# Quantised attention on one core: a projection's shift behind the exponentials on ACT, its clipping behind the rounding of the probabilities on DVE

## The reference, cut to what matters

```python
def _fq(x, delta, zp, n_bits):
    xi = _round_ste(x / delta) + zp
    xq = jnp.clip(xi, 0.0, 2.0 ** n_bits - 1.0)
    return (xq - zp) * delta
q = (x @ wq)...; k = (ctx @ wk)...; v = (ctx @ wv)...
sim = einsum(_fq(q, dq, 128.0, 8), _fq(k, dk, 128.0, 8)) * SCALE
attn = softmax(sim)
out = einsum(_fq(attn, dw, 0.0, 8), _fq(v, dv, 128.0, 8)) @ wo + bo
```

## Time and profile before

| | |
|---|---|
| time, median of 3 runs | 3130.22 us (3127.51 to 3131.3) |
| the profiled execution's own time | 3129.03 us |
| its span | 3127.2 us |
| PE busy | 2829.2 us, 90% |
| DVE busy | 1832.3 us, 59% |
| ACT busy | 1449.7 us, 46% |
| POOL busy | 706.1 us, 23% |
| L674 maximum | x256, mean 1219 ns |
| L688 scaling | x1024, mean 347 ns |
| L696 rounding | x256, mean 691 ns |
| L585 exponentials | x1024, mean 563 ns |
| L555 shift | x192, mean 778 ns |

### The profile page before, as it was taken

The page is one execution under the profiler, slowest core; times in us unless marked ns, Lnnn a source line. Parts: engine busy times, 40 slices in busy tenths (PEclk is TensorE's granted clock), DMA queues, the critical chain, the costliest instruction groups (busy, mean ns, idle before and its releaser), DMA issues. The chain is left out here.

```text
span 3127.2 us, 54588 instructions
## 1 busy us (share of the span) xinstructions
PE 2829.2 (90%) x18304; PEld 2274.0 (73%) x18304; DVE 1832.3 (59%) x4469; ACT 1449.7 (46%) x3747; POOL 706.1 (23%) x1147
## 2 busy tenths in 40 slices
PE   3689989989998886499999997999999999999997
PEld 2555666666565663289999997888888888888886
DVE  4599999999999997543333334334443344434332
ACT  3466677777667775321111112444444444444442
POOL 0122222222222222133333332111112111111110
PEclk8799999999999998699999998999999999999997
DMA  5133333333333333230000003000000000000000
GB/s 149 39 73 77 77 77 83 80 78 77 77 77 84 77 78 68 71 112 27 35 32 27 27 32 116 35 27 34 27 27 34 27 27 27 27 27 27 34 14 14
DMA packets 328217, 168.59 MB, mean 54 GB/s; under 512 B 276960, under 2 KB 293344, under 8 KB 328160
## 3 DMA queue, kind: packets, MB, share of 16 engines
q1 hardware_dynamic: 328160, 167.87, 21.1%
HBM read 75.54 MB, written 25.17 MB: 32 GB/s over the span
## 5 line engine op out<-in xcount | busy, mean ns | idle before, releaser
L585 ACT ACTIVATE e<-S,bias,qk_scale 128x256 f32<-128x256 f32 x1024 | 563.5, 563 | 106.9 <-DVE pq L696 100.2
L674 DVE TENSOR_REDUCE negmax<-S 128x4 f32<-128x1024 f32 x256 | 311.9, 1219 | 64.2 <-PE S L494 63.9
L688 DVE TENSOR_SCALAR e<-e,rsum 128x256 f32<-128x256 f32 x1024 | 291.0, 347 | 2.9
L555 ACT ACTIVATE shifted<-PJ,round_col,inv 128x512 f32<-128x512 f32 x192 | 149.2, 778 | 230.9 <-PE PJ L162 230.8
L153 PE MATMUL PJ<-w_a_wo,oT 128*128 128x512 f32 x512 | 243.7, 621 | 2.6 <-ACT oT L594 1.8
L1560 POOL TENSOR_TENSOR mid_partsB<-mid_actB,mid_partsB 128x256 fp32r<-128x256 f32 x128 | 101.4, 792 | 637.7 <-DVE mid_partsB L1465 637.7
L162 PE MATMUL PJ<-hT,w_a_wq 128*128 128x256 f32 x1536 | 202.7, 289 | 23.4 <-DVE w_a_wq L415 19.8
L162 PEld LDWEIGHTS PJ<-hT,w_a_wq 128*128 128x128 f32 x1536 | 190.5, 194 | 36.2 <-issue 36.2
L585 ACT ACTIVATION_READ_ACCUMULATOR e<-S,bias,qk_scale 128x1 f32 x1024 | 207.5, 203 | 0.0
L162 PE MATMUL AG0A<-h_partsA,upA 128*128 128x256 f32 x1536 | 200.2, 287 | 7.1 <-POOL h_partsA L1555 3.4
L162 PE MATMUL AG0B<-h_partsB,upB 128*128 128x256 f32 x1536 | 199.4, 286 | 7.3 <-POOL h_partsB L1555 6.2
(11 more groups left out here) (181 smaller groups left out, 5588.6 us busy)
## 6 DMA issues: line engine op xcount, KB each, us to landing
x_in<-in_x_dram SPq DMA_DIRECT2D x16, 512.0 KB, 3.6
ctx_in<-in_ctx_dram SPq DMA_DIRECT2D x16, 512.0 KB, 3.5
mid_dram<-x SPq DMA_DIRECT2D x16, 512.0 KB, 2.7
y_inA<-mid_dram SPq DMA_DIRECT2D x16, 512.0 KB, 3.5
part_dram<-x3A SPq DMA_DIRECT2D x16, 512.0 KB, 3.7
y_inB<-mid_dram SPq DMA_DIRECT2D x16, 512.0 KB, 3.2
kv_in<-in_ctx_dram SPq DMA_DIRECT2D x16, 512.0 KB, 4.6
baseB<-part_dram SPq DMA_DIRECT2D x16, 512.0 KB, 3.2
```

The costliest lines, as they stand in the source:

```text
L555: nc.scalar.activation(shifted[:, bank, :], PJ[bank][:], ACT.Identity, bias=round_col[:, 0:1], scale=inv[:, d:d + 1]).then_inc(pj_emptied[ ...
L585: nc.scalar.activation(e[:, s, i, :], S[s][:, i // 2, i % 2, :], ACT.Exp, bias=bias[:, s, i:i + 1], scale=qk_scale[:, ph.a:ph.a + 1], accu ...
L674: nc.vector.tensor_reduce(negmax[:, g % 2, :], S[g % 2][:].rearrange("p i q n -> p (i q) n"), AX_X, ALU.max, negate=True).then_inc(max_don ...
L688: nc.vector.tensor_scalar(e[:, s, i, :], e[:, s, i, :], rsum[:, s, i:i + 1], WMAX, ALU.mult, ALU.min).then_inc(prob_scaled, 1)
```

## The change

On ACT, in a step without transposes (`first` is false) the shifts are issued behind the exponentials; `oT` in steps 3 and 7 thereby also stands ahead of the shift. In a step with transposes nothing moves. On DVE, clip and unshift of every q, k or v filling go from their places inside the probabilities' chain to behind the rounding, back to back as `dve_quantise`. No instruction is added or left out.

```diff
                     if ph is P_A:
                         for c in chunks_beside(g):
                             act_weight_high(act, c)
-                    for where in late(ph, prev, g):
-                        if kind_of(where[2]) in QUANTISED:
-                            act_shift(act, where)
+                    shifts = [where for where in late(ph, prev, g) if kind_of(where[2]) in QUANTISED]
+                    first = bool(transposed(ph, g, 0))
+                    for where in shifts if first else ():
+                        act_shift(act, where)
                     if g == 7:
                         act_oT(act, ph, 0)
...
                     for where in transposed(ph, g, 0):
                         act_transposed(act, where)
                     act_exp(act, ph, g)
+                    for where in () if first else shifts:
+                        act_shift(act, where)
...
                 nc.vector.reciprocal(rsum[:, s, :], dsum[:, s, :]).then_inc(rsum_done, 1)
-                for where in fills:
-                    dve_clip(dve, where)
                 dve.wait_ge(rsum_done, n + 1)
...
-                for where in fills:
-                    dve_unshift(dve, where)
                 dve.wait_ge(prob_scaled, 4 * (n + 1))
...
                 nc.vector.tensor_scalar(pq[:, s], e[:, s], ROUND, ROUND, ALU.add,
                                         ALU.subtract).then_inc(prob_quantised, 1)
+                for where in fills:
+                    dve_quantise(dve, where)
```

## The result

The changed kernel takes 3202.1 us (median of 4 runs, 3200.5 to 3204.9) against 3128.9 before: a ratio of 1.0236 with an interval of 1.0221 to 1.0251. It is slower by 73 us where 18 were forecast, and outside the range of 3133 to 3163. The profiled execution has a span of 3201.4 us. The whole difference lies in the first part: the second part's first load comes at 1314.2 us before and at 1386.9 after, 72.7 us later.

The account below looks back on a forecast made before the run. PE's oT stalls were taken to set part of today's round, DVE to bound afterwards: 68.7 + 5.5 = 74.2 us. Fourteen rounds at 1.35 (+18.9), +2 for other fillings, -2.6 gave +18.3, 3148 us; range 3133 to 3163.

Parts of the forecast that it names:

- What bounds: First part's rounds of 72.80 us: PE's three 1.2 us waits for oT set part of the end; DVE idles behind them.
- What ACT's part gives: Shifts behind exponentials in 9 of 12 filling steps: up to 3.6 us of PE's time; DVE's waits for scores 4.1 us.
- The cover: Moved shifts cost nothing: DVE's clip comes last in its step, 2.6 + 0.6 us after the maximum starts, with the shift over.
- What DVE's part costs: Clip and unshift behind the rounding: 0.68 less 0.19 and 0.03, taken as 0.455 us a filling, 5.5 us a round.
- The sum: DVE's queue 68.7 + 5.5 = 74.2 us a round against 72.80, PE keeping up; together +18.3, giving 3148.
- the forecast's terms: Rounds of the first part: +1.35 us each, less 2.6 for two 74.1 us rounds whose longer PE wait DVE would swallow.
- 4.7 more: Outside the twelve rounds: the remaining rounds at +1.35 us each, and six fillings in P_B and P_Y taken as +2.
- every bound: Twelve fillings at 4.9 us a round give about 3141; at 6.1 with 0.5 us of PE waits left, 3168.
- The first: Faster rival: the place on DVE costs nothing, PE without oT waits bounds at 69.2 us a round, 3080; chance 0.10.
- the operations count: The Trainium skill's rule for DVE: count operations, not waits; reordering the same operations costs 0 instead of 5.5 us.
- The third: Slower rival: ACT's shifts free banks late, PE waits in up to nine steps; +14 on the forecast, 3162 and up; chance 0.06.

Follow-up runs that it names:

- e4: The kernel before with one edit on ACT: in steps 3 and 7 oT is made ahead of the shift; 3102.5 us, 0.9916.
- everything apart: Changed kernel, POOL's long side operations and first x_bo held until the unshift is done, normalised x between rounding and clip in phase2 step 7; 3138.0 us, 1.0031.
- e1: Changed kernel with POOL's long side operations (L779, L787, L799) held until that step's unshift is done instead of the rounding; 3148.9 us, 1.0064.

## Why the prediction was wrong

**What bounds: right.** PE's stalls at `oT` and DVE's idle behind them were read rightly, and e4 is that reading by itself: -26 us.

**What ACT's part gives: right in place.** PE's waits for `oT` fell from 3.6 to 0.9 us a round, DVE's seven waits went (4.1 us, as worked out), and no clip waited for ACT. PE waited for a shift only ahead of transposes, 1.1 us in two waits against 0.7 in one before. The cover that I had named, that the clip comes last, is shown by what happens without it (3271 us).

**What DVE's part costs: this step failed.** For the clip and unshift behind the rounding it said 0.68 us, from rows ahead of the loop. Where POOL is quiet that holds: over the loop's rounds the trace after has 0.45 and 0.21, and the gaps that close gave 0.23 for the 0.22 worked out, so the net is 0.43 us for 0.455, 5.2 us a round for 5.5. But the rows come from a place where POOL does nothing. In the loop POOL has four operations of 1.3 us a round whose release is the very rounding behind which the change puts DVE's two instructions. The unshift there takes 1.25 us and not 0.29, and its next instruction comes 1.18 us behind its start and not 0.21. That is 4 x 0.97 = 3.9 us a round, 54 us in fourteen rounds, and the run with POOL later takes back 53 of them. I costed the move on DVE's queue and on ACT's, and never read POOL's; its helper is called `pool_beside_max`, and the profile of before held a sign too, a clip of 0.52 us instead of 0.40 that overlapped one of these operations, once a round. Timelines of POOL and DVE before:

```profile
512.48 1.29 POOL L778 TENSOR_TENSOR x_bo<-x_in,r_a_bo 128x512 f32<-128x512 f32 x1 [1.32 <-DVE pq L696]
...
513.54 0.52 DVE L634 TENSOR_SCALAR rounded<-shifted 128x512 bf16<-128x512 f32 x1
```

The Trainium skill has the rule ("Advanced Engine Details and Errata", VectorE Performance Modes, Mode Summary): DVE's second SBUF port is shared with GpSimd, and instructions of DVE in a two-port mode and GpSimd's block each other. The traces agree: the bf16 unshift in SBUF is held, the maximum from PSUM is not. In the changed kernel POOL starts 0.2 to 0.3 us ahead of the unshift, which ends 0.15 us after POOL does; where the unshift starts first (the unshift alone behind the rounding) it is not held. That it is this port is the page's account; the runs show that the two collide and that the length of POOL's operation sets the loss.

**What was put at nothing: the clock.** The sum had no term for PE's clock. It costs the changed kernel about 0.9 us a round, as above; DVE's part alone, where DVE does not wait for the transposes, has rounds of 77.7 us for 78.5. Together with where x stands that is 11 us (3148.9 less 3138.0).

**The sum.** Measured by parts: +10 for the new order with everything apart (3138.0 less 3128.3), +11 for the clock and for where x stands, +53 for the collisions. The forecast had +18 for the new order and nothing for the other two. With everything apart the twelve rounds between loads take 10.3 us more than before, for 13.6 by the forecast's terms (12 x 1.35 less 2.6), and everything outside them came out 1 us shorter, where the forecast had 4.7 more: the fillings in P_B and P_Y cost nothing that can be seen. So the near agreement of e1 with the forecast, 3149 and 3148, is luck: 8 us too much for the order, 11 left out for the clock and the place of x.

**The rivals.** The first, that the place on DVE costs nothing, is refuted at 3138 with nothing else in the way; the operations count alone does not give the time, the gaps between them do. The third came nearest in time by another cause: PE waits for the shift hardly more than before. The range was too narrow because every bound was taken from DVE's, ACT's and PE's rows.

## What to carry to other kernels

When an instruction is moved to behind a semaphore's release, read who else is released by it and what they will run beside. A price taken from a quiet stretch of the trace holds only if the other engines are as quiet where the instruction goes; DVE's work in SBUF and POOL's need rows of their own. And take the parts of a change apart before judging it: here one line of it, `oT` ahead of the shift, was worth 26 us and was buried under 100.

## What had not been expected of the hardware

- A DVE instruction held by POOL shows as busy, not as idle: 1.27 us for one of 0.29, with no releaser. The minimum and maximum of a group's durations betray it (293 and 1271 ns for L647 in one round), and so does POOL's timeline beside it. POOL pays a little too, where it starts while the clip still runs: in the loop its L787 takes 1.31 to 1.41 us in the changed kernel, and the same operation 1.26 to 1.29 before.
- The dip of PE's clock is not tied to one wait or to one length of wait. With a wait of 2.4 us transposes took 1.09 us in some rounds of a run and 1.97 in others, with 1.63 us they took 1.8 in four of fourteen, with 3.1 us they were slow in most. Where they were fast, the dip often stood elsewhere in the same round, under a projection behind another of PE's waits. It costs a round up to 0.9 us where DVE has no lead and waits for PE, and nothing where it has. So the transposes alone do not tell whether a round had a dip; the granted clock of the whole round does.
- Scaling to rounding takes DVE 1.17 us for odd groups and 1.27 for even ones in most of the loop, 1.17 for both outside it. In the loop the wait ahead of the rounding has a value that the program works out at run time; that this is the cause is not shown.
